# A decoder layer on one core: the order of ScalarE's work in the transposed attention, two more banks for the first pair's exponentials, and another order of the drain

## The chip, the core and the metric

The kernel runs on one core of a Trainium2 chip. The metric is the device time of one execution in microseconds (us). PE is the matmul engine, ScalarE (ACT), VectorE (DVE) and GpSimd (POOL) do the element-wise work, SyncE (SP) issues loads. Data is in SBUF; matmuls write PSUM, which has banks of 512 float32 per partition.

## The reference, cut to what is computed

```python
x = x + _L0_attn_ref(_layernorm(x), ...)          # bidirectional minGRU, x is (4, 512, 256)
x = x + _L0_xattn_ref(_layernorm(x), ctx, Wq, Wk, Wv)
x = x + _L0_ffn_ref(_layernorm(x), ...)           # product keys, 16 of 256 experts for each of 8 heads

def _L0_xattn_ref(x, context, Wq, Wk, Wv):        # context is (4, 1601, 256)
    q = einsum('bsd,ed->bse', x, Wq); k = einsum('btd,ed->bte', context, Wk); v = einsum('btd,ed->bte', context, Wv)
    attn = softmax(einsum('bse,bte->bst', q, k) * 256 ** -0.5, axis=-1)
    return einsum('bst,bte->bse', attn, v)
```

The change touches only the second line, the attention over the context.

## The kernel before

Three stages follow each other, `stage_gru`, `stage_attention` and `stage_ffn`; each engine runs its own program of the three, written out in order by hand, and semaphores are the only links between engines. All that follows is `stage_attention` (lines 599 to 1256).

**Tiling.** The 2048 tokens are 16 tiles of 128, worked in 8 pairs `p` (256 columns), two pairs a batch. Scores are computed transposed: 128 context positions are the partitions, 256 tokens the columns. The 1601 context positions are 13 tiles in 7 groups `j` (six of two tiles, one short one of 65 rows), so a group fills one PSUM bank. Float32 is carried by two float32r halves, high and low: the high half is a ScalarE copy, the low half what VectorE or GpSimd subtracts, and every product is three matmuls (`split_products`, L75 to L77).

**A pair.** In the score phase PE computes `scores(p, j)` for the 7 groups into three banks in turn, 12 matmuls a group; VectorE keeps a running maximum (L965, L968) and ScalarE copies the bank to SBUF (`read_scores`, L852), after which the bank is free. The maximum is turned and spread by PE (L1149, L1157). In the exponential phase, for each group: VectorE subtracts the maximum into one of the same three banks (`shift_scores`, L997), ScalarE takes Exp in place (`raise_scores`, L859) and copies the high half to SBUF (`probs_high`, L867), VectorE subtracts for the low half (`probs_low`, L1005), after which the bank is free. Meanwhile PE computes the values of the pair before (`value_group(p - 1, j)`, L1177 to L1179, 12 matmuls a group). `probs_high(p, j)` waits for that value group, since it overwrites its operand. `scores(p + 1, 0)` waits until the fifth group of pair p is subtracted, `scores(p + 1, 1)` and `(.., 2)` for the sixth and seventh.

**What stands between.** PE has a ring of two more banks (`pR[:, 1]` and `pR[:, 2]`) for items: X (transposes of the normalised rows of the next batch, L1206), Q (queries of the next batch), V (transposes of a pair's values, L1217) and O (a tile's output product). `before_scores` and `behind_values` place them; each item waits until the item two before it is out of its bank, which VectorE does last (`low` L944, `output` L950). `read_values` (L835) takes a pair's values out of their banks. The context of the next batch comes in 47 pieces through four raw slots: SyncE loads, ScalarE copies the high half (`piece_high`, L842), GpSimd subtracts (`piece_low`, L806), and then the slot is loaded again. `UPTO` says how many pieces are done by the end of each pair.

**ScalarE's order before** is in the program below: four pieces of a pair stand between score copies 1 to 4, the others in the exponential phase; there, Exp of the next group stands ahead of the halving of this one, and the values are read behind the sixth halving. VectorE shifts three groups, and then alternates subtraction and shift.

**The drain** is what follows the exponential phase of the last pair: V and two O of pair 6, the value groups of pair 7 with X for the next stage between, and the first queries of the next stage.

## Time and profile before

| | us |
|---|---|
| time, median of 3 runs | 455.24 |
| lowest and highest | 454.93, 456.31 |
| the profiled execution | 455.93 |
| its span | 453.5 |
| exponential phases of pairs 0 to 7 begin at | 96.5, 124.2, 156.4, 184.4, 211.9, 241.0, 267.6, 297.2 |
| first queries of the next stage begin at | 327.0 |

Times of rows are us from the span's start. The attention stage takes PE from 82 to about 332 us. The page counts an engine as busy while an instruction of it runs; idle time is put down to whatever released the next instruction.

### The profile page before, as it was taken

The page shows a single profiled execution, that of the slowest core. Times are in us where ns is not written, and L with a number is a line of the kernel's source. Part 1 is how long each engine was busy: PE and PEld are TensorE (multiplying, and loading weights), DVE is VectorE, ACT ScalarE, POOL GpSimd, SP SyncE. Part 2 cuts the span into 40 slices and gives each one's busy share as a digit, 9 for nine tenths or more (in the row PEclk, how much of TensorE's full clock was granted, in tenths as well). Part 3 has the DMA queues.
Part 4 walks back from the last instruction along what each step waited for, and adds up shares of the span by engine and source line. Part 5 has one row for each costly group of instructions (what it writes and reads, how often), then busy time and mean ns, then how long its engine had stood idle before and what let it go on. Part 6 is the DMA issues. An engine that isn't in the chain of part 4 may idle for free.

```text
span 453.5 us, 8077 instructions
## 1 busy us (share of the span) xinstructions
PE 405.5 (89%) x2680; PEld 374.8 (83%) x2680; DVE 318.8 (70%) x1093; ACT 268.5 (59%) x575; POOL 213.3 (47%) x212
## 2 busy tenths in 40 slices
PE   8999999984977969969699796974999999999887
PEld 7788888974977969969699795974987899999776
DVE  5787867756674656776557666665168698899997
ACT  3886685455574565566645655442146797778653
POOL 2799999602314224133331330200015675989994
PEclk9999999995996989999889898995999996999999
DMA  8601321020501204012130220000000000001011
GB/s 244 235 1 30 91 69 30 0 74 21 147 23 30 72 25 120 24 54 72 48 100 20 55 72 1 1 0 0 1 25 2 0 2 0 14 26 37 23 37 58
DMA packets 19992, 21.38 MB, mean 47 GB/s; under 512 B 3180, under 2 KB 16624, under 8 KB 19952
## 3 DMA queue, kind: packets, MB, share of 16 engines
q1 hardware_dynamic: 18832, 19.96, 15.0%
q10 hardware_dynamic: 1120, 0.92, 0.7%
q8 instruction: 21, 0.34, 0.3%
q14 instruction: 19, 0.16, 0.1%
HBM read 18.78 MB, written 2.10 MB: 46 GB/s over the span
## 4 chain that ended last, share of the span: by engine, by line
PE 57%; DVE 12%; POOL 10%; issue 8%; ACT 8%; DMA 2%; SPq 1%; ACTq 0%; DVEq 0%; POOLq 0%
PE keep_pQ L75 10%; PE keep_pQ L76 10%; PE keep_pQ L77 10%; POOL ffn_prod L1410 8%; DVE keep_pQ L997 5%; ACT att_pTh L867 5%; DVE att_pTl L1005 4%; ACT keep_pQ L859 3%; PE context_pR L534 2%; PE context_pA L534 2%; POOL ffn_near L1478 2%; DMA gru_wa<-in_xWk 2%; PE ffn_pK L1959 2%; PE ffn_pT L1989 1%; PE context_pR L1206 1%
## 5 line engine op out<-in xcount | busy, mean ns | idle before, releaser
L859 ACT ACTIVATE keep_pQ<-keep_pQ 128x512 f32<-128x512 f32 (+1 forms) x56 | 31.0, 553 | 58.7 <-DVE keep_pQ L997 58.6
L1005 DVE TENSOR_TENSOR att_pTl<-keep_pQ,att_pTh 128x512 fp32r<-128x512 f32 (+1 forms) x56 | 36.4, 652 | 39.8 <-ACT att_pTh L867 39.7
L852 ACT ACTIVATE att_prob<-keep_pQ 128x512 f32<-128x512 f32 (+1 forms) x56 | 31.4, 568 | 42.0 <-DVE att_most L965 15.7
L1410 POOL TENSOR_TENSOR ffn_prod<-ffn_first,ffn_near 128x1024 f32<-128x1024 f32 (+1 forms) x29 | 54.2, 1887 | 2.1 <-DVE ffn_first L1836 2.1
L75 PE MATMUL keep_pQ<-keep_qT0h,context_cTh 128*128 128x256 f32 (+1 forms) x104 | 32.4, 312 | 14.1 <-DVE att_pTl L1005 14.1
L75 PE MATMUL keep_pQ<-keep_qT0h,att_cTh 128*128 128x256 f32 (+1 forms) x104 | 33.2, 319 | 12.1 <-DVE att_pTl L1005 12.1
L968 DVE TENSOR_TENSOR att_most<-att_most,keep_pQ 128x512 f32<-128x512 f32 (+1 forms) x40 | 25.3, 633 | 23.4 <-PE keep_pQ L77 22.2
L997 DVE TENSOR_TENSOR keep_pQ<-att_prob,keep_pQ 128x512 f32<-128x512 f32 (+1 forms) x56 | 34.9, 649 | 6.5 <-PE keep_pQ L1157 6.5
L806 POOL TENSOR_TENSOR att_cNl<-keep_raw,att_cNh 128x512 fp32r<-128x512 f32 (+1 forms) x14 | 15.8, 1125 | 41.9 <-ACT att_cNh L842 41.9
L1989 PE MATMUL ffn_pT<-keep_ident,ffn_prod 128*128 128x128 f32 x240 | 30.4, 283 | 3.8 <-POOL ffn_prod L1410 3.8
L75 PEld LDWEIGHTS keep_pQ<-keep_qT0h,context_cTh 128*128 128x128 f32 (+1 forms) x104 | 21.3, 205 | 14.9 <-DVE att_pTl L1005 14.9
L1989 PEld LDWEIGHTS ffn_pT<-keep_ident,ffn_prod 128*128 128x128 f32 x240 | 28.6, 148 | 5.9 <-DVE ffn_hT L1869 4.9
L75 PEld LDWEIGHTS keep_pQ<-keep_qT0h,att_cTh 128*128 128x128 f32 (+1 forms) x104 | 21.7, 209 | 12.9 <-DVE att_pTl L1005 12.9
L76 PE MATMUL keep_pQ<-keep_qT0l,att_cTh 128*128 128x256 f32 (+1 forms) x104 | 31.7, 305 | 0.0
L77 PE MATMUL keep_pQ<-keep_qT0h,att_cTl 128*128 128x256 f32 (+1 forms) x104 | 31.6, 304 | 0.0
L867 ACT ACTIVATE att_pTh<-keep_pQ 128x512 fp32r<-128x512 f32 (+1 forms) x56 | 31.4, 563 | 0.0
L77 PE MATMUL keep_pQ<-keep_qT0h,context_cTl 128*128 128x256 f32 (+1 forms) x104 | 31.1, 299 | 0.0
L76 PE MATMUL keep_pQ<-keep_qT0l,context_cTh 128*128 128x256 f32 (+1 forms) x104 | 31.0, 298 | 0.0
L806 POOL TENSOR_TENSOR att_cTl<-keep_raw,att_cTh 128x512 fp32r<-128x512 f32 (+1 forms) x16 | 15.3, 971 | 31.7 <-ACT att_cTh L842 31.7
L1798 DVE MAX8 ffn_top<-ffn_e 128x8 f32<-128x32 f32 x256 | 29.3, 177 | 0.4 <-ACT ffn_e L1598 0.2
L235 POOL TENSOR_TENSOR gru_z<-gru_z,gru_g 128x512 f32<-128x512 f32 x16 | 26.5, 1656 | 6.4 <-DVE gru_g L414 5.7
L429 DVE TENSOR_TENSOR_SCAN gru_hT<-gru_c,gru_z 128x512 f32<-128x512 f32 x16 | 24.4, 1524 | 3.8 <-POOL gru_z L235 3.8
(356 smaller groups left out, 1413.0 us busy)
## 6 DMA issues: line engine op xcount, KB each, us to landing
keep_raw<-in_ctxT SPq DMA_DIRECT2D x24, 256.0 KB, 2.6
keep_raw<-in_ctx SPq DMA_DIRECT2D x24, 256.0 KB, 2.8
out<-keep_x SPq DMA_DIRECT2D x16, 128.0 KB, 1.7
keep_x<-in_x SPq DMA_DIRECT2D x3, 512.0 KB, 11.1
gru_wout<-in_W_out SPq DMA_DIRECT2D x1, 512.0 KB, 9.0
keep_raw<-in_fWq SPq DMA_DIRECT2D x2, 256.0 KB
keep_raw<-in_ctxT SPq DMA_DIRECT2D x8, 32.5 KB, 3.0
keep_raw<-in_ctx SPq DMA_DIRECT2D x4, 65.0 KB
```

The costliest lines, as they stand in the source:

```text
L75: pe.matmul(out, lh, rh, start=(i == 0), stop=False)
L76: pe.matmul(out, lh, rl, start=False, stop=False)
L77: last = pe.matmul(out, ll, rh, start=False, stop=(i == n - 1))
L806: pool.tensor_tensor(lo, raw(i % RAW), hi.bitcast(F32), ALU.subtract).then_inc(piece_lo, 1)
L852: act.activation(prob[0:rows(j), GROUPS[j][0]:GROUPS[j][-1] + 1].rearrange("p c n -> p (c n)"), pS[0:rows(j), score_bank(p, j), 0:n * COLS ...
L859: act.activation(e, e, ACT.Exp, scale=ATT_SCALE).then_inc(raised, 1)
L867: act.activation(to, pS[0:rows(j), exp_bank(p, j), 0:len(GROUPS[j]) * COLS], ACT.Copy).then_inc(prob_high, 1)
L997: dve.tensor_tensor(e, s, shift[0:rows(j)].unsqueeze(1).broadcast_to([rows(j), n, COLS]), ALU.subtract)\
L1005: dve.tensor_tensor(pT[1][0:rows(j), which], e, pT[0][0:rows(j), which].bitcast(F32), ALU.subtract)\
L1410: return eng.tensor_tensor(prod[:, i % PB, a:b].rearrange("p h (i j) -> p h i j", j=KEYS), (factor if factor is not None else first[:, n % ...
L1798: ins = dve.max(top[:, n % 2, t, h, a:a + 2 * TOPK], e[:, n % 2, t, h, half * KEYS:(half + 1) * KEYS])
L1989: last = pe.matmul(pW[:, i % 2, c * P:(c + 1) * P], prod[:, i % PB, h, c * P:(c + 1) * P], ident[:], start=(h == 0), stop=(c == 0 and h == ...
```

## The change

Five edits in `stage_attention`; no instruction is added or taken away.

- ScalarE in the exponential phase does Exp and halving of one group, then of the next, instead of Exp one group ahead; the values of the pair before are read behind the fifth halving instead of the sixth.
- ScalarE's pieces stand behind score copies 0 to 4, and what is left of a pair's pieces ahead of its first Exp; none is left in the exponential phase, save in pair 0. GpSimd's roots stand ahead of all pieces of their pair.
- In pairs 2 and 4 the items X stand one score group later.
- In pair 0, groups 4 and 5 are shifted into `pR[:, 0]` and `pR[:, 1]`, which are idle then; what waits for a bank of pair 0 waits for its last user in the new order. VectorE's two residual additions of that pair move towards its end.
- In the drain V(6), O(12), O(13) stand between the value groups of pair 7, and X of the next stage two groups later; ScalarE and VectorE follow in the same order.

```diff
@@ before_scores, behind_values
-        if j in (2, 3) and p in (1, 2, 4, 7):
-            out.append(("X", {1: 1, 2: 2, 4: 3, 7: 4}[p], j - 2))
+        if p in (1, 2, 4, 7):
+            first = 2 if p % 2 else 3
+            if j in (first, first + 1):
+                out.append(("X", {1: 1, 2: 2, 4: 3, 7: 4}[p], j - first))
...
         if p == PAIRS:
-            return {3: [("X", BATCH + 1, 0)], 4: [("X", BATCH + 1, 1)]}.get(j, [])
+            return {1: [("V", PAIRS - 2, 0)], 3: [("O", TILES - 4, 0)], 4: [("O", TILES - 3, 0)],
+                    5: [("X", BATCH + 1, 0)], 6: [("X", BATCH + 1, 1)]}.get(j, [])
@@ banks of the first pair; SPARE = (4, 5)
     def exp_bank(p, j):
-        return (2 * NG * p + NG + j) % BANKS
+        if p == 0 and j in SPARE:
+            return pR[:, SPARE.index(j)]
+        return pS[:, (2 * NG * p + NG + j) % BANKS]
+
+    def last_exp(p, j):
+        if p == 0:
+            return (1, 2, 6)[j]
+        return NG - BANKS + j
@@ scalar
         for p in range(PAIRS):
-            early, late = early_pieces(p), late_pieces(p)
+            left = list(pieces_at(p))
             for j in range(NG):
...
                 read_scores(p, j)
-                if early and j in (1, 2, 3, 4):
-                    piece_high(early.pop(0))
-            raise_scores(p, 0)
+                if p and j < 5 and left:
+                    piece_high(left.pop(0))
+            if p:
+                for i in left:
+                    piece_high(i)
             for j in range(NG):
-                if j + 1 < NG:
-                    raise_scores(p, j + 1)
+                raise_scores(p, j)
                 probs_high(p, j)
...
-                if p >= 1 and j == 5:
+                if p >= 1 and j == 4:
                     read_values(p - 1)
-                if p and j in (2, 4, 5) and late:
-                    piece_high(late.pop(0))
-            for i in late:
-                piece_high(i)
-        high(("V", PAIRS - 2, 0))
+            if p == 0:
+                for i in left:
+                    piece_high(i)
@@ vector
-            else:
+            elif p or j not in SPARE:
                 dve.wait_ge(prob_low, NG * p + j - BANKS + 1)
...
-                if p == 0 and j in (2, 4):
-                    last_residual((j - 2) // 2)
+                if p == 0 and j == 5:
+                    last_residual(0)
+            if p == 0:
+                last_residual(1)
@@ tensor
-                pe.wait_ge(prob_low, NG * (p - 1) + NG - BANKS + j + 1)
+                pe.wait_ge(prob_low, NG * (p - 1) + last_exp(p - 1, j) + 1)
...
+            if n == 0:
+                pe.wait_ge(prob_low, SPARE[1] + 1)
...
-        item(("V", PAIRS - 2, 0))
-        item(("O", TILES - 4, 0))
-        item(("O", TILES - 3, 0))
         for j in range(NG):
             value_group(PAIRS - 1, j)
             for it in behind_values(PAIRS, j):
```

ScalarE's program through the exponential phase of pair 2, before. L859 is Exp in place, L867 the halving, L842 a piece, L835 the reads of the values:

```order
L852 ACTIVATE att_prob<-keep_pQ 65x256
L859 ACTIVATE keep_pQ<-keep_pQ 128x512 x2
L867 ACTIVATE att_pTh<-keep_pQ 128x512
L859 ACTIVATE keep_pQ<-keep_pQ 128x512
L867 ACTIVATE att_pTh<-keep_pQ 128x512
L859 ACTIVATE keep_pQ<-keep_pQ 128x512
L867 ACTIVATE att_pTh<-keep_pQ 128x512
L842 ACTIVATE context_cTh<-keep_raw 128x512
L859 ACTIVATE keep_pQ<-keep_pQ 128x512
L867 ACTIVATE att_pTh<-keep_pQ 128x512
```

The same place in the changed kernel, where these lines are L856, L863, L871 and L846, through the third group:

```order
L856 ACTIVATE att_prob<-keep_pQ 65x256
L846 ACTIVATE context_cTh<-keep_raw 128x512 x2
L846 ACTIVATE context_cTh<-keep_raw 128x65
L863 ACTIVATE keep_pQ<-keep_pQ 128x512
L871 ACTIVATE att_pTh<-keep_pQ 128x512
L863 ACTIVATE keep_pQ<-keep_pQ 128x512
L871 ACTIVATE att_pTh<-keep_pQ 128x512
L863 ACTIVATE keep_pQ<-keep_pQ 128x512
L871 ACTIVATE att_pTh<-keep_pQ 128x512
```

The two Exp at the head are now one, and three pieces stand ahead of it.

VectorE's program in the exponential phase of pair 0, before. L997 is the shift, L1005 the subtraction, L1031 the residual addition:

```order
L1005 TENSOR_TENSOR att_pTl<-keep_pQ,att_pTh 128x512
L997 TENSOR_TENSOR keep_pQ<-att_prob,keep_pQ 128x512
L1031 TENSOR_TENSOR keep_x<-context_pR,keep_x 128x512
L1005 TENSOR_TENSOR att_pTl<-keep_pQ,att_pTh 128x512
L997 TENSOR_TENSOR keep_pQ<-att_prob,keep_pQ 128x512
L1005 TENSOR_TENSOR att_pTl<-keep_pQ,att_pTh 128x512
L997 TENSOR_TENSOR keep_pQ<-att_prob,keep_pQ 65x256
L1031 TENSOR_TENSOR keep_x<-context_pA,keep_x 128x512
L1005 TENSOR_TENSOR att_pTl<-keep_pQ,att_pTh 128x512
L1005 TENSOR_TENSOR att_pTl<-keep_pQ,att_pTh 65x256
```

The same place in the changed kernel, where these lines are L1001, L1009 and L1035:

```order
L1009 TENSOR_TENSOR att_pTl<-keep_pQ,att_pTh 128x512
L1001 TENSOR_TENSOR context_pR<-att_prob,keep_pQ 128x512
L1009 TENSOR_TENSOR att_pTl<-keep_pQ,att_pTh 128x512
L1001 TENSOR_TENSOR context_pR<-att_prob,keep_pQ 128x512
L1009 TENSOR_TENSOR att_pTl<-context_pR,att_pTh 128x512
L1001 TENSOR_TENSOR keep_pQ<-att_prob,keep_pQ 65x256
L1009 TENSOR_TENSOR att_pTl<-context_pR,att_pTh 128x512
L1035 TENSOR_TENSOR keep_x<-context_pR,keep_x 128x512
L1009 TENSOR_TENSOR att_pTl<-keep_pQ,att_pTh 65x256
L1035 TENSOR_TENSOR keep_x<-context_pA,keep_x 128x512
```

Shift and subtraction alternate as before; two groups lie in `context_pR`, and the residuals stand behind them.

PE's program at the start of the drain, before (L1177 to L1179 are values, L1217 is V, and L75 to L77 here are O):

```order
L1177 MATMUL context_pR<-att_cNh,att_pTh 128x258
L1178 MATMUL context_pR<-att_cNh,att_pTl 128x258
L1179 MATMUL context_pR<-att_cNl,att_pTh 128x258
L1217 MATMUL context_pR<-keep_ident,att_vn 128x128 x4
L75 MATMUL context_pR<-keep_WvTh,att_vTh 128x256
L76 MATMUL context_pR<-keep_WvTl,att_vTh 128x256
```

In the changed kernel V (L1226) has a value group of pair 7 (L1184 to L1186) ahead of it and behind it:

```order
L1184 MATMUL context_pR<-att_cNh,att_pTh 128x258
L1185 MATMUL context_pR<-att_cNh,att_pTl 128x258
L1186 MATMUL context_pR<-att_cNl,att_pTh 128x258
L1226 MATMUL context_pR<-keep_ident,att_vn 128x128 x4
L1184 MATMUL context_pA<-att_cNh,att_pTh 128x258
L1185 MATMUL context_pA<-att_cNh,att_pTl 128x258
```

V no longer stands directly behind the last value group of pair 6, and O no longer directly behind V.

## Rows read from the trace of the kernel before

**Rows 1.** The page, part 1: busy us, share of the span, instructions.

```profile
PE 405.5 (89%) x2680; PEld 374.8 (83%) x2680; DVE 318.8 (70%) x1093; ACT 268.5 (59%) x575; POOL 213.3 (47%) x212
```

**Rows 2.** The waits: engine, line, waited for; us in total, times, longest.

```profile
ACT keep_pQ L859 <- DVE keep_pQ L997: 58.6, 40, 3.3
PE keep_pQ L75 <- DVE att_pTl L1005: 26.1, 7, 8.1
PE context_pR L1217 <- ACT att_vn L835: 7.1, 2, 6.9
PE context_pR L1206 <- DVE att_xn L936: 4.1, 2, 3.0
```

**Rows 3.** Timeline of VectorE, pair 2; start us, us, engine, line, operation:

```profile
138.27 0.42 DVE L1005 TENSOR_TENSOR att_pTl<-keep_pQ,att_pTh 65x256 fp32r<-65x256 f32 x1 [0.64 <-ACT att_pTh L867]
...
156.43 1.89 DVE L997 TENSOR_TENSOR keep_pQ<-att_prob,keep_pQ 128x512 f32<-128x512 f32 x3 [0.98 <-PE keep_pQ L1157]
...
160.48 0.69 DVE L997 TENSOR_TENSOR keep_pQ<-att_prob,keep_pQ 128x512 f32<-128x512 f32 x1
...
162.32 0.69 DVE L1005 TENSOR_TENSOR att_pTl<-keep_pQ,att_pTh 128x512 fp32r<-128x512 f32 x1 [1.15 <-ACT att_pTh L867]
...
167.22 0.69 DVE L1005 TENSOR_TENSOR att_pTl<-keep_pQ,att_pTh 128x512 fp32r<-128x512 f32 x1 [1.15 <-ACT att_pTh L867]
```

**Rows 4.** Timeline of ScalarE, pair 2:

```profile
161.20 0.58 ACT L859 ACTIVATE keep_pQ<-keep_pQ 128x512 f32<-128x512 f32 x1 [1.36 <-DVE keep_pQ L997]
161.70 0.59 ACT L867 ACTIVATE att_pTh<-keep_pQ 128x512 fp32r<-128x512 f32 x1
```

**Rows 5.** Timeline of PE at the starts of pairs and of the drain:

```profile
108.06 0.58 PE L75 MATMUL keep_pQ<-keep_qT0h,context_cTh 128*128 128x256 f32 x1 [8.11 <-DVE att_pTl L1005]
...
143.91 1.09 PE L1206 MATMUL context_pR<-keep_ident,att_xn 128*128 128x128 f32 x4 [3.02 <-DVE att_xn L936]
...
163.40 0.28 PE L75 MATMUL context_pR<-keep_WvTh,att_vTh 128*128 128x256 f32 x1
163.52 0.28 PE L76 MATMUL context_pR<-keep_WvTl,att_vTh 128*128 128x256 f32 x1
...
167.96 0.58 PE L75 MATMUL keep_pQ<-keep_qT0h,att_cTh 128*128 128x256 f32 x1 [3.69 <-DVE att_pTl L1005]
...
195.93 0.39 PE L75 MATMUL keep_pQ<-keep_qT0h,context_cTh 128*128 128x256 f32 x1 [2.30 <-DVE att_pTl L1005]
...
313.18 0.55 PE L75 MATMUL context_pR<-keep_WvTh,att_vTh 128*128 128x256 f32 x1 [1.52 <-DVE att_vTl L944]
```

**Rows 6.** Windows; length, busy PE, PEld, DVE, ACT, POOL, granted clock, DMA, GB/s.

```profile
108.06:113.58 5.52, 5.52 (x28) 5.52 (x29) 3.67 (x13) 3.31 (x8) 3.48 (x3) 0.55 0.18 47
135.73:140.89 5.16, 5.16 (x28) 4.80 (x28) 3.25 (x12) 3.27 (x8) 2.37 (x3) 0.67 0.23 64
143.91:147.65 3.74, 3.74 (x21) 3.74 (x21) 1.28 (x4) 1.60 (x3) 1.18 (x1) 0.56 0.02 4
167.96:171.24 3.28, 3.28 (x17) 3.28 (x17) 2.10 (x6) 2.66 (x8) 2.06 (x2) 0.52 0.28 77
195.93:199.83 3.90, 3.73 (x28) 3.34 (x28) 2.33 (x6) 3.16 (x8) 2.20 (x2) 1.00 0.20 67
223.44:229.37 5.93, 5.93 (x28) 5.93 (x29) 3.18 (x9) 3.53 (x9) 2.65 (x3) 0.52 0.33 94
252.51:257.44 4.93, 4.93 (x28) 4.93 (x29) 1.96 (x4) 3.39 (x8) 2.19 (x2) 0.65 0.27 67
279.09:284.56 5.47, 5.09 (x28) 4.58 (x28) 4.38 (x13) 2.87 (x7) 0.00 (x0) 0.69 0.00 0
310.57:318.21 7.64, 6.12 (x29) 5.74 (x30) 4.45 (x15) 0.72 (x2) 0.39 (x1) 0.52 0.00 0
```

**Rows 7.** Timeline of GpSimd, the first four pieces:

```profile
110.10 4.04 POOL L806 TENSOR_TENSOR att_cTl<-keep_raw,att_cTh 128x512 fp32r<-128x512 f32 x4 [9.88 <-ACT att_cTh L842]
```

**Rows 8.** Loads by line: engine, operation, count, KB each, median us to landing.

```profile
keep_raw<-in_ctxT SPq DMA_DIRECT2D x24, 256.0 KB, 2.6
```

36 lines of the change are left out of this document (16 added, 20 removed).

## The prediction, made before the changed kernel ran

> **What bounds the kernel now.** I read first the page's busy times: PE is busy 405.5 us of the 453.5 us span, ScalarE 268.5 [rows 1]. So PE is the engine to fill, and the question is where its remaining time goes and at what clock it runs. The waits answer the first [rows 2]: the first scores of a pair waited 26.1 us in seven places for VectorE's subtraction L1005, the drain 7.1 us for ScalarE's reads of the values, the transposes of X 4.1 us for normalised rows; on the other side ScalarE's Exp waited 58.6 us in 40 places for VectorE's shift L997. Engines that are idle for each other in turn, while PE waits for the last of it: the exponential phase is a ring of latencies, not of work.
>
> The timeline of pair 2 shows the ring [rows 3, 4]. Write S(j) for the shift of group j, E(j) for Exp, H(j) for the halving copy, L(j) for the subtraction. VectorE ran S0, S1, S2 from 156.43; S3 began 160.48; E3 161.20 (0.72 behind S3, and ScalarE had been idle 1.36); H2 161.70 (0.50 behind E3, since H(j) stands behind E(j+1)); L2 162.32 (0.62); the next S comes one step of VectorE's queue after it, 0.60 to 0.61 (three shifts take 1.89, one 0.69). The turn is 0.72 + 0.50 + 0.62 + 0.61 = 2.45 us a group, and L4 began at 156.43 + 10.79 = 167.22. PE's last value group ended at 163.40, an output product of six matmuls followed to about 164.1, and pair 3 started at 167.96, after 3.69 idle [rows 5]. After such an idle stretch the granted clock is low: 0.52 to 0.69 over the first stretches of pairs 1 to 3, 5 to 7 and of the drain, 1.00 only behind one wait of 2.3 us [rows 6]; half the full 2.4 GHz is the 1.2 GHz level.
>
> **The change, part by part.**
>
> *ScalarE goes bank by bank* (E0 H0 E1 H1 ...). H(j) now stands right behind E(j) and waits for its result. No row shows an Exp followed by its own dependant. Its price lies between the issue step 0.50 and the duration plus a hand-over; an Exp lasts 0.58 [rows 4], and L follows H by 0.62 across engines, so I take 0.62, the upper neighbour. VectorE's order stays S0 S1 S2 L0 L1 S3 L2 S4 L3 S5 L4 S6 L5 L6, but S(j+1) is now done while ScalarE works on j. Counting from S0: E0 0.73, H0 1.35, L0 1.98; E1 1.84, H1 2.46, L1 3.09, S3 3.70; E2 2.95, H2 3.57, L2 4.31 (behind S3), S4 4.92; E3 4.43, H3 5.05, L3 5.68, S5 6.29; E4 5.65, H4 6.27, L4 6.90. So 1.29 us a group where there were 2.45, and L4 at +6.90 instead of +10.79. PE's values of the pair before end at 163.40, +7.0, in even pairs, and with an output product at +7.7; where two Q products lie between, PE's idle time was 2.30 instead of 3.69 [rows 5], so it is free 1.4 later, at +9.1. L4 is through at +7.65: the 26.1 us of waits at a pair's first scores go, save in the first pair. At 0.50 for the unseen step L4 comes 0.3 earlier and nothing more is won; at 0.8 it comes 0.5 later and costs even pairs 0.5 each.
>
> *What is late next.* The reads of the values move from behind H5 to behind H4. They wait for PE's last value group (+7.13 with its tail), take 0.27 each (estimated: half a copy step of 0.50, since they have half the columns), and E5, H5, E6, H6 stand behind them: E5 7.69, H5 8.31, L5 8.94, then the output O5 of even pairs on VectorE, done 10.07. PE has the next pair's first bank (1.4, 12 matmuls of 0.12 [rows 5]) from 7.7 to 9.1, and then its transposes of the values need O5's bank: 0.97 us of waiting. In odd pairs L5 is done 11.79 and PE is free 10.83: 0.96. So six transitions keep 0.97 each, 5.8 in all.
>
> *Pieces between score copies.* Each pair has up to five of its 7 or 8 context pieces at score copies 0 to 4 and the rest ahead of E0, where ScalarE was idle for up to 3.3 us [rows 2]. A piece is 0.5 of ScalarE's queue, and a step of the score phase is 1.4 to 1.8 of PE, so copy and piece (1.0) and even an X copy (1.5) fit. The fifth piece needs the raw slot of the first: 0.7 to GpSimd, 1.1 there (4.04 for three and a short one [rows 7]), 2.6 to load [rows 8], some 4.4, and it comes 7 us later. Hidden. If loads took three times as long it would no longer be.
>
> *X one copy later in pairs 2 and 4.* In pair 2 X came at 143.91, 5.64 behind L6 at 138.27 [rows 3, 5]: moments, GpSimd's root, four scalings. With L6 at +11.7 they come at +17.35; PE is ready at 14.6, so 2.7 us of its wait stays there, and the lower clock behind it (some 1.3). In pair 4 the wait goes. In pair 7, where X was not moved, the chain on VectorE is L6 at +9.95, O6 10.3, moments from 10.7, four scalings from 11.8 to 13.3 (steps as behind L6 in pair 2, without the root), and PE is ready at 11.85: 1.45 us, new.
>
> *First pair.* Groups 4 and 5 go to two idle banks, so pair 1's first two banks wait only for L1 and L2. S0 of pair 0 was 11.53 ahead of 108.06 (10.79, and 0.74 until the product), at 96.5, and L1 is now through at 96.53 + 3.84 = 100.4; PE was free at 108.06 - 8.11 = 99.95 [rows 5]. Waits that remain: 0.4; then X needs L5 (105.5) when PE is free at 103.2, 2.35; bank 2 needs L6 (106.5), behind which stand a residual, 0.55; and PE's fifth bank waits for ScalarE's second copy, which stands behind the fifth piece, whose load lands at about 109.9 (GpSimd's first piece starts about 4 us before 110.10 [rows 7] and takes 1.1; 2.6 more and ScalarE's hand-over), 1.5; turning the maxima 0.1. Together 4.9, and 0.4 of slow clock (little, since the fifth bank waits anyway).
>
> *Drain.* V(6), O, O now stand between the value groups of pair 7. They had cost 7.1 and 1.52 of idle PE [rows 2, 5]; in their place only value group 0 waits for the reads behind H4: 7.45 against 6.3, 1.2. All else has its operands, since V(6)'s halves are ready 1 us ahead of O.
>
> *Sum.* Taken away: 26.1 + 7.1 + 4.1 + 1.5 = 38.8 of waits; at each of the 12 waits another 0.16, since a matmul is shown 0.28 long and the next could start after 0.12: 1.9; and the low clock, one minus the granted share times the length of the stretches of rows 6: 2.5 + 1.7 + 1.65 + 1.6 + 0 + 2.85 + 1.7 + 1.7 + 2.9 (on its busy 6.1 us) = 16.6. Together 57.3. Left or new: 4.9 + 5.8 + 2.7 + 1.45 + 1.2 = 16.05, and 1.7 of clock: 17.75. Gain 39.5. The profiled execution took 455.93 us, so 416.4; it stood 0.7 above the median of 455.24, which makes 415.7.
>
> The clock term is the softest. Each pair still has a gap of about 1 us. Gaps of 2.33, 2.30 and 2.33 were followed by 0.67, 1.00 and 0.65 [rows 6]. None as short as 1 us stands in front of a slow stretch in these rows, so I let the clock stay high. The Trainium skill (TensorE: Matmul & The Clock Gate, section A second HAM failure mode) tells of a kernel that cycles through PSUM banks and idles briefly between groups of matmuls often enough that the clock swings between its two levels; by that rule the kernel would keep much of its 16.6 us, and the time would be near that of the second rival. No row here shows it without a wait of over 2 us ahead.
>
> **The rivals.**
>
> 1. *The ring turns slower than worked out:* E and H on ScalarE and S and L on VectorE all touch PSUM at once, or the step E to H costs 0.8 or more. Before, the pairs of them overlapped too, and durations stayed at 0.58 to 0.61 and 0.69, which speaks against it. At 0.2 to 0.3 more a group, L4 and the tail each come about 0.7 later in seven places: 5 us, 420.7.
>
> 2. *The clock still falls at the transitions.* For it: two of three gaps of 2.3 us did it, and the new gap stands close to the next one at X. Against it: work of 1.4 us now lies between. Price by rows 6: 1.6 us (the stretch at 167.96) in seven places, 11 us: 427.
>
> 3. *The moved pieces block the score copies,* and the kernel becomes slower. Place: copy 4 of pairs 1 to 5, behind it on ScalarE the copies on which PE's next banks wait. It decides from a load of 8 us (slack 5.6 beyond the 2.6 shown is 3); to eat 39.5 us over five pairs the fifth piece must come 7.9 us late each time, a load near 14 us. At 15 us: 5 x 9.4 = 47, and 463. Speaks against it: 2.6 us median over 24 loads [rows 8].
>
> 4. *The change doesn't do what it says:* H(j) is held by something else, such as PE's value groups, and the ring stays 2.45. H waits for the same value group as before; group 3 ends at 2.8 and 4 at 4.3 in even pairs, ahead of H. Then only X, drain and pieces count: some 14 us, 441.
>
> 5. *More is won:* no loss in the first pair (the load lands early) and no slow clock at all, 411.
>
> **How the numbers follow.** Forecast 415.7, own range 412 to 419: 0.60. Rival 1: 0.12; rival 2: 0.12; rival 3: 0.03; rival 4: 0.04; rival 5: 0.07; the rest, 0.02, no change. From 409 to 427.5 the range leaves out rivals 3 and 4, the rest and the ends. About 0.3% (1.4 us) is what a measurement of this kernel can tell from no change; every case but rival 3 and the rest is faster: 0.95, same 0.02, slower 0.03.
>
> **What would show it.** L4 begins 6.9 us behind S0 (was 10.8), H(j) starts 0.62 behind E(j). PE's wait for L1005 falls from 26.1 to about 6, most of it at the second bank of a pair instead of the first. The reads of the values after H4 wait for PE's value group. PE waits about 2.7 at X in pair 2 and 1.5 at X in pair 7. The drain runs without a wait over 1.5 us. The granted clock is 1.00 through the first banks of pairs 3 to 7. I am wrong in size if the first banks stay at 0.5 to 0.7 of the clock, and in kind if ScalarE idles in front of copy 4 for a piece's load.

## The result, and the profile after

The changed kernel took 417.92 us (median of 3 runs, 417.60 to 418.93) against 455.24 before: 0.918 of the time, 95% interval 0.9146 to 0.9214. The forecast was 415.7, its range 412 to 419. The profiled execution took 418.93 us with a span of 416.6, and is to be set against 455.93 and 453.5: 37.0 us less by the times and 36.9 by the spans, where the sum gave 39.5.

First the busy times, to be read against [rows 1], and the waits, against [rows 2] (engine, line, what it waited for; us in total, times, longest):

```profile
PE 390.8 (94%) x2680; PEld 357.8 (86%) x2680; DVE 321.1 (77%) x1093; ACT 271.3 (65%) x575; POOL 213.9 (51%) x212
```

```profile
ACT keep_pQ L863 <- DVE keep_pQ L1001: 21.7, 13, 3.3
PE context_pR L1215 <- DVE att_xn L940: 4.4, 2, 3.3
PE keep_pQ L75 <- DVE att_pTl L1009: 2.9, 5, 0.8
PE context_pR L1226 <- DVE keep_x L954: 2.5, 3, 0.8
PE context_pR L1215 <- DVE att_pTl L1009: 2.1, 1, 2.1
PE keep_pQ L1156 <- DVE att_top L979: 1.2, 1, 1.2
```

PE's wait for the subtraction at a pair's start (L1005 before, L1009 now) fell from 26.1 us to 2.9, its longest from 8.1 to 0.8; ScalarE's Exp waited for the shift 40 times before and 13 now. PE's busy time fell by 14.7 us at the same number of instructions, most of it by the clock. Of that, 11.8 us lie in the attention, from pair 0's first shift to the first queries of the next stage, first before and then changed (start and end; length, busy PE, PEld, DVE, ACT, POOL, granted clock, DMA, GB/s):

```profile
96.53:327.03 230.50, 191.20 (x1402) 185.28 (x1401) 142.47 (x285) 120.97 (x245) 54.03 (x54) 0.90 0.16 44
96.39:291.64 195.25, 179.40 (x1403) 172.50 (x1401) 141.47 (x279) 123.02 (x244) 53.70 (x53) 0.99 0.18 51
```

The shorter windows, to be read against [rows 6] (same columns): pair 7's first banks, the stretch behind pair 2's wait for X, and the drain:

```profile
253.94:258.40 4.46, 3.64 (x30) 3.29 (x28) 3.30 (x11) 3.49 (x8) 1.29 (x1) 1.00 0.00 0
138.57:143.90 5.33, 5.33 (x34) 5.33 (x35) 2.99 (x6) 3.73 (x8) 2.42 (x3) 0.70 0.35 97
279.60:285.00 5.40, 5.40 (x45) 5.40 (x46) 3.51 (x10) 2.19 (x5) 0.00 (x0) 1.00 0.00 0
```

Of eleven such stretches of the attention, at the places of rows 6 and behind the new waits, ten stand at 1.00 and one at 0.70.

The ring of the exponential phase, pair 6, first VectorE, then ScalarE (start us, us, engine, line, operation):

```profile
246.27 1.89 DVE L1001 TENSOR_TENSOR keep_pQ<-att_prob,keep_pQ 128x512 f32<-128x512 f32 x3 [0.98 <-PE keep_pQ L1164]
...
249.97 0.69 DVE L1001 TENSOR_TENSOR keep_pQ<-att_prob,keep_pQ 128x512 f32<-128x512 f32 x1
...
253.14 0.68 DVE L1009 TENSOR_TENSOR att_pTl<-keep_pQ,att_pTh 128x512 fp32r<-128x512 f32 x1
...
255.24 0.69 DVE L1009 TENSOR_TENSOR att_pTl<-keep_pQ,att_pTh 128x512 fp32r<-128x512 f32 x1 [1.09 <-ACT att_pTh L871]
```

```profile
247.00 0.58 ACT L863 ACTIVATE keep_pQ<-keep_pQ 128x512 f32<-128x512 f32 x1 [3.29 <-DVE keep_pQ L1001]
247.61 0.60 ACT L871 ACTIVATE att_pTh<-keep_pQ 128x512 fp32r<-128x512 f32 x1
248.11 0.59 ACT L863 ACTIVATE keep_pQ<-keep_pQ 128x512 f32<-128x512 f32 x1
...
253.43 0.39 ACT L839 ACTIVATE att_vn<-context_pA 128x258 f32<-128x258 f32 x1 [0.33 <-PE context_pR L1186]
```

The halving starts 0.61 behind its Exp, and the fifth subtraction 6.87 behind the first shift (253.14 - 246.27); in the kernel before it was 10.79 [rows 3]. In pairs 1, 3 and 5, where two query products stand between, it is 7.88.

Where the 36.9 us of span went, by the starts of the exponential phases: from that of pair 0 to that of pair 7 it was 200.6 us (297.17 - 96.53) and is 175.7 (272.07 - 96.39), 25.0 less; from there to the first queries of the next stage 29.8 and 19.5, 10.3 less; the next stage 1.5 less; up to pair 0, 0.1. The change doesn't touch the next stage. In the kernel before, the profiled execution has a stretch of 6.8 us at half the clock there (from 375.88) and the stage takes 126.5 us; the changed kernel has none and takes 125.0. The stage takes 126.3 to 126.6 us also in the profiles of `a1_exp_ahead`, `b4_read_late` and `d2_all`, and 124.9 in that of `a2_order_only`. So these 1.5 us come and go between profiled kernels; none of the edits is shown to cause them.

### The profile page after: what moved, and what is told of

Read it like the earlier page. It is cut to its first block, busy times and chain, and to the rows that moved or that the text cites. A ratio compares the mean times of both kernels' runs of the same rounds, so it can differ in the third digit from the quotient of the medians.

```text
span 416.6 us, 8078 instructions
## 1 busy us (share of the span) xinstructions
PE 390.8 (94%) x2680; PEld 357.8 (86%) x2680; DVE 321.1 (77%) x1093; ACT 271.3 (65%) x575; POOL 213.9 (51%) x212
## 4 chain that ended last, share of the span: by engine, by line
PE 67%; POOL 12%; DVE 8%; ACT 5%; issue 5%; DMA 2%; ACTq 0%; DVEq 0%; POOLq 0%
PE keep_pQ L75 10%; PE keep_pQ L77 9%; PE keep_pQ L76 9%; POOL ffn_prod L1416 8%; PE context_pR L534 3%; PE context_pA L1184 3%; PE context_pA L534 2%; PE context_pR L1186 2%; PE context_pR L1184 2%; PE context_pA L1186 2%; PE context_pA L1185 2%; PE context_pR L1185 2%; POOL ffn_near L1484 2%; ACT att_pTh L871 2%; ACT keep_pQ L863 2%
## 5 line engine op out<-in xcount | busy, mean ns | idle before, releaser
L856 ACT ACTIVATE att_prob<-keep_pQ 128x512 f32<-128x512 f32 (+1 forms) x56 | 31.2, 564 | 35.4 <-PE keep_pQ L77 10.5
L1009 DVE TENSOR_TENSOR att_pTl<-keep_pQ,att_pTh 128x512 fp32r<-128x512 f32 (+1 forms) x54 | 34.9, 647 | 14.9 <-ACT att_pTh L871 13.9
L863 ACT ACTIVATE keep_pQ<-keep_pQ 128x512 f32<-128x512 f32 (+1 forms) x54 | 30.3, 560 | 21.7 <-DVE keep_pQ L1001 21.7
L972 DVE TENSOR_TENSOR att_most<-att_most,keep_pQ 128x512 f32<-128x512 f32 (+1 forms) x40 | 25.3, 631 | 19.5 <-PE keep_pQ L77 18.2
L1001 DVE TENSOR_TENSOR keep_pQ<-att_prob,keep_pQ 128x512 f32<-128x512 f32 (+1 forms) x54 | 33.5, 648 | 5.7 <-PE keep_pQ L1164 5.7
L75 PE MATMUL keep_pQ<-keep_qT0h,context_cTh 128*128 128x256 f32 (+1 forms) x104 | 30.3, 291 | 2.8 <-DVE att_pTl L1009 1.4
L1995 PEld LDWEIGHTS ffn_pT<-keep_ident,ffn_prod 128*128 128x128 f32 x240 | 26.8, 141 | 6.6 <-DVE ffn_hT L1875 4.9
L871 ACT ACTIVATE att_pTh<-keep_pQ 128x512 fp32r<-128x512 f32 (+1 forms) x54 | 30.5, 566 | 2.8 <-PE context_pR L1186 1.2
L75 PE MATMUL keep_pQ<-keep_qT0h,att_cTh 128*128 128x256 f32 (+1 forms) x104 | 30.7, 295 | 1.5 <-DVE att_pTl L1009 1.5
L805 POOL TENSOR_TENSOR keep_rstd<-att_ve,keep_mhalf 128x4 f32<-128x4 f32 x3 | 3.3, 1089 | 56.0 <-DVE att_ve L1100 31.9
L76 PE MATMUL keep_pQ<-keep_qT0l,att_cTh 128*128 128x256 f32 (+1 forms) x104 | 29.7, 285 | 0.0
L77 PE MATMUL keep_pQ<-keep_qT0h,att_cTl 128*128 128x256 f32 (+1 forms) x104 | 29.6, 285 | 0.0
L77 PE MATMUL keep_pQ<-keep_qT0h,context_cTl 128*128 128x256 f32 (+1 forms) x104 | 29.2, 281 | 0.0
L76 PE MATMUL keep_pQ<-keep_qT0l,context_cTh 128*128 128x256 f32 (+1 forms) x104 | 29.1, 280 | 0.0
L75 PE MATMUL keep_pQ<-gru_xTh,gru_wh 128*128 128x512 f32 x56 | 24.0, 428 | 0.0
L75 PEld LDWEIGHTS keep_pQ<-keep_qT0h,context_cTh 128*128 128x128 f32 (+1 forms) x104 | 19.1, 184 | 4.2 <-DVE att_pTl L1009 2.3
## 6 DMA issues: line engine op xcount, KB each, us to landing
keep_x<-in_x SPq DMA_DIRECT2D x3, 512.0 KB, 10.3
```

The lines of the kernel that those rows point to most:

```text
L75: pe.matmul(out, lh, rh, start=(i == 0), stop=False)
L76: pe.matmul(out, lh, rl, start=False, stop=False)
L77: last = pe.matmul(out, ll, rh, start=False, stop=(i == n - 1))
L856: act.activation(prob[0:rows(j), GROUPS[j][0]:GROUPS[j][-1] + 1].rearrange("p c n -> p (c n)"), pS[0:rows(j), score_bank(p, j), 0:n * COLS ...
L863: act.activation(e, e, ACT.Exp, scale=ATT_SCALE).then_inc(raised, 1)
L871: act.activation(to, exp_bank(p, j)[0:rows(j), 0:len(GROUPS[j]) * COLS], ACT.Copy).then_inc(prob_high, 1)
```

## Experiments

Ratios are to the kernel before, measured beside it on the same chip; the changed kernel's is 0.918 (0.9146 to 0.9214). All through this section, "phases" is the time from the start of pair 0's exponential phase to that of pair 7 in the profiled execution: 200.6 us before, 175.7 changed. It leaves the drain out and shows smaller differences than the medians do, but it comes from one execution of each. "L5" and "L6" below are the sixth and seventh subtraction of a pair, as in the prediction.

### The order of ScalarE, undone and alone

`a1_exp_ahead`, changed kernel:

```diff
+            raise_scores(p, 0)
             for j in range(NG):
-                raise_scores(p, j)
+                if j + 1 < NG:
+                    raise_scores(p, j + 1)
                 probs_high(p, j)
```

> The changed kernel with one thing undone: ScalarE again raises group j + 1 before it halves group j; pieces, spare banks, reads and drain stay as changed. Theory (the order Exp, halving of one bank is what the change is worth): the shift of group j + 2 waits again for a bank that is one Exp longer in coming, the last subtraction of a pair moves from 6.87 us behind the first shift back towards 10.8, that is up to 3.9 us in each of 8 pairs, and the granted clock falls again behind the longer gaps on TensorE: 440 to 450 us. Rival (what ScalarE no longer does between the exponentials, pieces and reads, is what shortened them): at most 5 us is lost, 418 to 423 us.

450.62 us, ratio 0.9897 (0.9849 to 0.9946), 0.6 above the theory's range: 32.7 of the 37.3 us are gone with these lines (450.62 - 417.92). VectorE, pair 6:

```profile
268.81 1.89 DVE L1003 TENSOR_TENSOR keep_pQ<-att_prob,keep_pQ 128x512 f32<-128x512 f32 x3 [0.98 <-PE keep_pQ L1166]
...
279.60 0.69 DVE L1011 TENSOR_TENSOR att_pTl<-keep_pQ,att_pTh 128x512 fp32r<-128x512 f32 x1 [1.15 <-ACT att_pTh L871]
```

279.60 - 268.81 = 10.79, what the kernel before had, though neither pieces nor reads changed places. The rival (what ScalarE no longer does between the exponentials) is refuted. The granted clock of the run is 0.95 again. From pair 0's first shift to the next stage's first queries PE stands still for 35.1 us in place of 15.9, and is busy 14.0 us longer: more than half of what the order brings is waiting, and nearly all of the rest is the clock that falls behind the waits (159 matmuls start at the lower level there, 15 in the changed kernel).

`a2_order_only`, kernel before:

```diff
-            raise_scores(p, 0)
             for j in range(NG):
-                if j + 1 < NG:
-                    raise_scores(p, j + 1)
+                raise_scores(p, j)
                 probs_high(p, j)
```

> The kernel before with one thing done: ScalarE halves each group right behind its Exp. Pieces still stand between the exponentials and between the score copies 1 to 4, the reads of the values behind the last halving, pair 0 has no spare banks, and the drain is as before. Theory: the order alone brings most of the gain, less the pieces of ScalarE that stand in the exponential phase (three, some 0.6 us each) and the old drain (some 9 us): 426 to 436 us. Rival (order and pieces are only worth something together): over 440 us.

423.79 us, ratio 0.9311 (0.9275 to 0.9347): below the range of the theory. The order alone brings 31 us (0.069 of 455). Its phases take 172.8 us (269.41 - 96.59), 2.9 less than with all five edits. From pair 0 to pair 7, the other edits cost more than they bring. What it lacks stands in the drain (PE's waits):

```profile
278.31 1.09 PE L1215 MATMUL context_pR<-keep_ident,att_vn 128*128 128x128 f32 x4 [2.45 <-ACT att_vn L835]
281.32 0.55 PE L75 MATMUL context_pR<-keep_WvTh,att_vTh 128*128 128x256 f32 x1 [1.92 <-DVE att_vTl L942]
```

### The other edits, undone one at a time

`a3_pieces_back`, changed kernel, ScalarE's pieces in their old places:

```diff
-                if p and j < 5 and left:
+                if p and j in (1, 2, 3, 4) and left:
                     piece_high(left.pop(0))
...
                     read_values(p - 1)
+                if p and j in (2, 4, 5) and left:
+                    piece_high(left.pop(0))
```

> The changed kernel with ScalarE's pieces put back: behind the score copies 1 to 4 and behind the halvings 2, 4 and 5. Theory (each piece in the exponential phase lengthens it by its own duration, since ScalarE and VectorE now wait for each other there): of the three, the two in front of the fifth subtraction cost about 0.6 us each in the pairs that still have seven pieces: 2 to 6 us slower than the changed kernel. Rival (it is hidden by the ring of two banks): within 1 us of it.

418.54 us, ratio 0.9204 (0.9171 to 0.9236): no difference. Its phases take 174.6 us, 1.0 less. The theory is half right: in pairs 1, 3 and 5 L5 and L6 come later (11.58 and 12.78 behind the first shift, against 11.06 and 11.74), in pairs 2 and 4 by 0.5 and 0.7, and PE waits 1.16 to 1.27 us at the turns behind these five pairs and not 0.73 to 0.84. What makes up for it is the step from pair 0 to pair 1, 22.1 us against 24.0. There, and in the pairs behind, the way from the maximum over the groups to the first shift is 2.82 to 2.94 us, where the changed kernel has 3.2 to 3.7 in pairs 1 to 5. That led to the runs on GpSimd below.

`a4_drain_back`, changed kernel, the drain as before:

```diff
         if p == PAIRS:
-            return {1: [("V", PAIRS - 2, 0)], 3: [("O", TILES - 4, 0)], 4: [("O", TILES - 3, 0)],
-                    5: [("X", BATCH + 1, 0)], 6: [("X", BATCH + 1, 1)]}.get(j, [])
+            return {0: [], 3: [("X", BATCH + 1, 0)], 4: [("X", BATCH + 1, 1)]}.get(j, [])
...
+    ring += [("V", PAIRS - 2, 0), ("O", TILES - 4, 0), ("O", TILES - 3, 0)]
     for j in range(NG):
         ring += behind_values(PAIRS, j)
```

(and each engine's program follows that order).

> The changed kernel with the drain as before: the values of pair 6 and their two outputs stand whole ahead of pair 7's values, and the X products of the last tiles behind values 3 and 4. Theory, from the prediction's terms for the drain: TensorE waits 9 to 12 us more there in all (8.11 and 3.02 us were the two longest waits of this kind in the kernel before), the clock with it: 426 to 431 us. Rival (the next waits of the drain are late enough to take most of it back): under 3 us slower.

426.00 us, ratio 0.9373 (0.9334 to 0.9412), 8.1 us over the changed kernel by the medians; by the profiled spans 6.2, of which 5.1 lie behind pair 7's first shift and 1.3 in pair 2, where the low clock behind the X product lasts longer. The expectation took 8.11 and 3.02, which were waits of pairs 1 and 2, for those of the drain, 6.94 and 1.52. PE's waits in the drain come to 4.6 us against 1.07, 3.5 more and not 9 to 12, since with the faster ring V(6) waits 1.07 us and not 6.94; the wait that is left is for V's low half:

```profile
284.81 0.55 PE L75 MATMUL context_pR<-keep_WvTh,att_vTh 128*128 128x256 f32 x1 [3.52 <-DVE att_vTl L949]
```

`b1_no_spare`, changed kernel, no spare banks:

```diff
-        if p == 0 and j in SPARE:
-            return pR[:, SPARE.index(j)]
         return pS[:, (2 * NG * p + NG + j) % BANKS]
```

(and the waits for the banks' last users follow).

> The changed kernel without the two idle banks for pair 0's exponentials: groups 4 and 5 shift into the ring of three like the others. Theory: subtraction 4 of pair 0 comes some 1.5 to 2.5 us later and TensorE, which has little other work there, waits for it: 1.5 to 4 us slower than the changed kernel. Rival (the X products and the value products behind hide it): within 0.5 us.

418.98 us, ratio 0.9213 (0.9180 to 0.9246); phases 175.75 us, as in the changed kernel. By the phases the rival holds. PE waits once for a subtraction there, ahead of pair 1's first scores:

```profile
103.45 0.50 PE L75 MATMUL keep_pQ<-keep_qT0h,context_cTh 128*128 128x256 f32 x1 [4.18 <-DVE att_pTl L1005]
```

With the two banks it waits 0.42, 2.05, 0.27, 1.09 and 0.25 us in turn, 4.08 in all. The edit splits a wait and removes next to nothing.

`b2_x_back`, changed kernel:

```diff
-            first = 2 if p % 2 else 3
+            first = 2
```

> The changed kernel with the X products of pairs 2 and 4 one group earlier, where they stood before. Theory: the X product of pair 2, which waits 3.31 us for the scaled tile already, waits one group (about 1.4 us) longer, and pair 4's about as long as pair 7's (1.10 us): 1.5 to 4 us slower. Rival (TensorE waits less later for the same subtractions): within 0.7 us.

421.74 us, ratio 0.9265 (0.9234 to 0.9297), 3.8 us over by the medians; phases 177.6 us, 1.9 over. X in pair 2 waits 4.74 us in place of 3.31. By either measure the size is in the theory's range. Of the 1.9 us, 1.5 come in pair 2 and 0.4 in pair 4.

### What delays the first shift

The changed kernel's VectorE, and GpSimd at the same times:

```profile
116.63 1.32 DVE L979 TENSOR_TENSOR att_top<-att_most 128x256 f32<-128x256 f32 x1
...
136.20 2.22 DVE L940 TENSOR_SCALAR att_xn<-keep_x,keep_mv,att_rstd 128x256 f32<-128x256 f32 x4 [1.76 <-POOL att_rstd L799]
...
172.27 1.01 DVE L987 TENSOR_TENSOR att_diag<-keep_ident,att_mx 128x256 f32<-128x256 f32 x1
```

```profile
116.49 2.50 POOL L812 TENSOR_TENSOR att_cNl<-keep_raw,att_cNh 128x512 fp32r<-128x512 f32 x2 [1.59 <-ACT att_cNh L846]
...
136.13 1.18 POOL L812 TENSOR_TENSOR att_cNl<-keep_raw,att_cNh 128x512 fp32r<-128x512 f32 x1
...
171.81 2.51 POOL L812 TENSOR_TENSOR context_cNl<-keep_raw,context_cNh 128x512 fp32r<-128x512 f32 x2 [1.43 <-ACT context_cNh L846]
```

Where no piece of GpSimd runs beside them, the maximum over the groups (L979) and the diagonal (L987) take 0.42 us and the four scalings (L940) 1.38. In the kernel before, all eight maxima and all eight diagonals took 0.42 to 0.43; two of those maxima ran beside GpSimd's root of four values per partition, none beside a piece. Each long one begins inside a piece and ends behind it: the piece of 136.13 ends at 137.31, and the first scaling, begun at 136.20, took 1.26 us and not 0.40. The shifts, which read one operand in PSUM, keep their 1.89 for three beside the same pieces. So do the statistics of a tile, which read one operand in SBUF; this one runs inside the piece of 172.95 to 174.31:

```profile
173.20 0.41 DVE L959 BATCH_NORM_STATS2 att_stats<-keep_x 128x6 f32<-128x256 f32 x1
```

The Trainium skill (SBUF — State Buffer, section Who interferes with whom) has this: VectorE and GpSimd share one pair of SBUF ports as an exclusive lock, and a VectorE operation with two SBUF inputs contends with a GpSimd operation that reads SBUF. This trace agrees with it for the maximum and the diagonal: 0.72 to 1.32 us for the seven that began well inside a piece, and 0.42 to 0.43 for the others. The scalings read one tensor and two values per partition, and the first of them was held as well. To test that GpSimd's pieces are the cause, GpSimd alone was held:

`b3_hold_low`, changed kernel:

```diff
-            for i in pieces_at(p):
+            for n, i in enumerate(pieces_at(p)):
+                if p and n == 5:
+                    pool.wait_ge(shifted, NG * p + 1)
+                if p == 2 and n == 0:
+                    pool.wait_ge(xn_ready, 2)
                 piece_low(i)
```

> The changed kernel, except that GpSimd holds its leftover pieces (the sixth and seventh of a pair) until the first shift of that pair is done, and its first piece of pair 2 until the four scalings of that pair are done. No instruction is added on any computing engine. Theory (what was missed: VectorE's operations with two inputs in SBUF stand still while GpSimd works on SBUF; the maximum over the groups took 1.32 and 0.80 us beside pieces against 0.42, the diagonal 0.72 to 1.02 against 0.42, four scalings 2.22 against 1.38): these go back to 0.42 and 1.38 us, the way from the top to the first shift from 3.2 to 3.7 us back to 2.9, 2.5 to 3.2 us in all: 414.7 to 415.5 us. Rival (they are longer for another reason, such as reads of PSUM by both): the durations stay and the time with them, 417.9 us. Rival (held pieces come late for TensorE or hold the next pair): slower than the changed kernel.

416.94 us, ratio 0.9160 (0.9131 to 0.9189): by the medians not to be told from the changed kernel. Its phases take 174.0 us, 1.7 less. VectorE in pair 2:

```profile
135.98 1.38 DVE L944 TENSOR_SCALAR att_xn<-keep_x,keep_mv,att_rstd 128x256 f32<-128x256 f32 x4 [1.76 <-POOL att_rstd L799]
...
145.73 0.81 DVE L983 TENSOR_TENSOR att_top<-att_most 128x256 f32<-128x256 f32 x1
...
147.53 0.43 DVE L991 TENSOR_TENSOR att_diag<-keep_ident,att_mx 128x256 f32<-128x256 f32 x1
```

Scalings and diagonal are back to 1.38 and 0.43. The maximum over the groups stays at 0.81, and at 1.32 in pair 1: beside it runs the fifth piece (144.96 to 146.24 in pair 2), which this kernel doesn't hold. So the hold was placed one piece too late, and brought 1.7 us of the 2.5 to 3.2 expected. The mechanism stands: what GpSimd no longer runs beside is back to its length, and what it still runs beside is not.

### The reads of the values, and the clock

`b4_read_late`, changed kernel:

```diff
-                if p >= 1 and j == 4:
+                if p >= 1 and j == (4 if p == PAIRS - 1 else 5):
                     read_values(p - 1)
```

> The changed kernel, except that ScalarE reads the values of the pair before behind the last halving in pairs 1 to 6, and not behind the fifth. Theory (the five reads stand ahead of the sixth Exp, and VectorE waits 2.2 us there for the halving): the sixth subtraction comes earlier by the reads, and TensorE's wait of 0.75 to 0.97 us for it at each turn of pairs goes: up to 5 us faster, 413 to 415 us. Rival (the value products that wait for the two banks that the reads free come to stand in its place): between 0 and 3 us slower.

413.74 us, ratio 0.9092 (0.9060 to 0.9123), 4.2 us faster than the changed kernel; phases 171.0 us, 4.7 less. L5 comes 8.24 us behind the first shift in pairs 2, 4 and 6 (was 8.97) and about 9.2 in pairs 1, 3 and 5 (was 11.06); PE's waits of 0.73 to 0.84 at the second bank are gone. But X in pair 7 now waits 1.62 (was 1.10), since PE is there earlier. Reading the values behind H4, a part of the change, is a loss in pairs 1 to 6.

`c1_fill`, changed kernel:

```diff
+            if it == ("X", 2, 0):
+                pe.wait_ge(shifted, 2 * NG)
+                for _ in range(FILLS):
+                    pe.matmul(turned[:, 0], ident[:], ident[:], start=True, stop=True)
```

> The changed kernel with 12 more matmuls of the identity by itself in front of pair 2's first X product, started when the last shift of pair 1 is done, into a bank nobody reads; they fill the 3.31 us in which TensorE stands still there and compute nothing that is used. Theory (the granted clock of 0.70 between 138.57 and 143.90 us follows from that idle time): the clock stays 1.00 in the stretch behind it, which gives back some 1.6 us: 416 to 417 us. Rival (the clock falls there for another reason, or filling costs as much as it gives): the 0.70 stays, 417.9 us or up to 1 us more.

417.13 us, ratio 0.9163 (0.9133 to 0.9193); not to be told from the changed kernel by the medians, so the trace decides. The stretches in and behind the filled wait:

```profile
135.30:138.20 2.90, 2.35 (x22) 2.16 (x21) 2.58 (x5) 0.00 (x0) 1.43 (x2) 1.00 0.15 26
138.20:143.50 5.30, 5.30 (x48) 5.30 (x47) 4.27 (x9) 4.70 (x10) 3.13 (x3) 1.00 0.33 92
```

1.00 where there was 0.70, and 28.19 us from pair 1's first shift to pair 2's against 29.66: 1.5 us, as the clock term says. One execution could be chance, so the others count too: in each of the ten other profiled executions in which PE waits at this place (2.47 to 4.74 us) the clock falls to half there, and in `d1`, `d2` and `d3` below, where the wait is gone, it doesn't. The low clock there follows from the idle time and not from what runs behind it. The same profile has a low stretch that the changed kernel's has not, in pair 1, behind a first X product that waited equally long (2.05 and 2.04 us). Changed kernel, then this one:

```profile
105.37:111.31 5.94, 4.58 (x35) 4.13 (x36) 4.53 (x13) 3.32 (x8) 4.93 (x5) 1.00 0.39 97
```

```profile
104.73:110.20 5.47, 5.20 (x30) 4.96 (x31) 4.54 (x13) 3.10 (x7) 4.33 (x5) 0.69 0.37 96
```

It costs nothing visible (24.02 us from pair 0's first shift to pair 1's, against 23.96), since the wait for a score copy behind it, 1.09 us in the changed kernel, is gone in exchange.

### Towards a faster kernel

`d1_moments_early`, changed kernel: the statistics of the last four tiles leave the end of pair 1:

```diff
+                if p == 1:
+                    early_moments(j)
...
-            if p in (0, 1):
-                left_moments(2 + p)
-            if p == 1:
-                dve.tensor_scalar(ve[:, 2 * TPB:], mv2[:, 2 * TPB:, 1], LN_EPS, None, ALU.add).then_inc(ve_ready, 1)
+            if p == 0:
+                left_moments(2)
```

(`early_moments`: two statistics each at j = 3 and 4, aggregates and L1080's addition at j = 5.)

> The changed kernel with one thing moved on VectorE: the statistics of the last four tiles, which stand between pair 1's last subtraction and pair 2 (four at 130.81 us, the aggregates, the root on GpSimd behind them, 1.76 us of waiting for it), go between the maxima of groups 3 to 5 of pair 1. Theory (the 3.31 us wait of pair 2's X product is this chain): the four scalings stand directly behind pair 1's last subtraction, the wait goes to under 0.5 us and the clock of the stretch behind it to 1.00: 413 to 414.5 us. Rival (the X product then waits for something else, or the maxima of pair 1 come late by as much): 416 us or more.

415.87 us, ratio 0.9123 (0.9094 to 0.9152): a part of what the theory gave. The wait in pair 2 is gone, and from pair 1's first shift to pair 2's it is 24.8 us (was 29.7). But the step from pair 0 to pair 1 grew from 24.0 to 26.7. The clock fell to half there and pair 1's diagonal met a piece (1.01 us), but first of all VectorE now came late to the turn of the maxima:

```profile
PE keep_pQ L1173 <- DVE att_top L979: 2.4, 1, 2.4
```

`d2_all`: that, the late reads of b4, X one group later in pairs 1 and 7 (`first = 3`), and b3's hold from the fifth piece on (`n == 4`).

```diff
-            first = 2 if p % 2 else 3
+            first = 3
...
+                if p and n == 4:
+                    pool.wait_ge(shifted, NG * p + 1)
...
-                if p >= 1 and j == 4:
+                if p >= 1 and j == (4 if p == PAIRS - 1 else 5):
```

> The changed kernel with all that the runs so far point to: statistics early as in the run before, values read behind the last halving in pairs 1 to 6, X products of pairs 1 and 7 one group later, and GpSimd holding the fifth to seventh piece of a pair until that pair's first shift is done, so that none of them runs beside the maximum over the groups and the diagonal. Theory (the terms add): 4.2 us for the reads, 3.5 to 4.5 us for the statistics, 1.5 to 3 us for the held pieces, 1 to 3 us for the waits of 2.05 and 1.10 us in front of the X products: 404 to 409 us. Rival (one wait takes the place of another): 410 to 413 us.

411.75 us, ratio 0.9039 (0.9016 to 0.9062): by the rival's range. The terms don't add: the same lateness in pair 1 (2.5) stays, and PE's wait at score group 2 of pair 1 is 2.98. Moving X in pairs 1 and 7 brought nothing: in pair 1 the 2.98 stands in place of 2.05 and 0.27, and in pair 7 PE now waits twice for the same ring of two banks, in front of the output products, where `b4_read_late` waited 1.62 once:

```profile
254.50 0.39 PE L75 MATMUL context_pR<-keep_WvTh,att_vTh 128*128 128x256 f32 x1 [1.17 <-DVE keep_xT0l L952]
...
258.26 0.38 PE L75 MATMUL context_pR<-keep_WvTh,att_vTh 128*128 128x256 f32 x1 [1.38 <-DVE keep_xT0l L952]
```

From pair 6's first shift to pair 7's it is 27.2 us, against 25.6 in `b4_read_late`.

`d3_spread`: d2_all with VectorE's work around pair 1 spread:

```diff
+                if p == 1 and j in (2, 3):
+                    early_moments(at, 3 * TPB + 2 * (j - 2), 2)
...
+            if p == 0:
+                last_residual(0)
+                last_residual(1)
```

(with the first four tiles' statistics at the maxima 1 to 3 of pair 1.)

> The run before (d2_all) with VectorE's work around pair 1 spread out. There, the statistics between the maxima of pair 1 made TensorE wait 2.47 us for the maximum over the groups, and the last subtraction of pair 0 at 105.46 us, behind one half of the last residual, made it wait 2.98 us. Now both halves of that residual stand behind pair 0's last subtraction, the statistics of the first four of the eight tiles between the maxima of groups 1 to 3 of pair 1 (VectorE stood idle 1.36 and 1.86 us there), and those of the last four between the subtractions 2 to 4 of pair 1, beside TensorE's query products. Theory (VectorE has room there, and the waits were its lateness): 0.6 us less in front of score group 2 of pair 1, up to 2 us less in front of the turned maxima: 408.5 to 410.5 us. Rival (the ring of pair 1 has no room, and the statistics only move the wait to pair 1's last subtractions): 411 to 413 us.

411.06 us, ratio 0.9038 (0.9009 to 0.9068): 0.7 below d2_all by the median and equal by the interval; the phases are 167.1 us against 169.0. The profiled execution took 410.32, in the theory's range, the median not. It is the fastest kernel here by the median, 1.6% under the changed one, and it keeps the 27.3 us from pair 6 to pair 7: by the 25.6 of `b4_read_late`, leaving X where it was in pair 7 should give another 1.7 us (an estimate, not run). Of its waits on PE and of VectorE in pair 2:

```profile
PE keep_pQ L75 <- DVE att_pTl L1013: 3.6, 3, 2.5
PE keep_pQ L1179 <- DVE att_top L983: 1.1, 1, 1.1
```

```profile
141.67 0.43 DVE L983 TENSOR_TENSOR att_top<-att_most 128x256 f32<-128x256 f32 x1
...
143.19 0.43 DVE L991 TENSOR_TENSOR att_diag<-keep_ident,att_mx 128x256 f32<-128x256 f32 x1
```

With the fifth piece held too, the maximum over the groups is back to 0.43, which b3 had left open.

## Why the prediction was right, and where it was off

**The ring: right.** The measured 417.92 us lies in the range of 412 to 419, 2.2 above the forecast, and for the reason given. The step from Exp to halving was 0.61 (0.62 taken), the fifth subtraction at +6.87 (6.90). a1 and a2 show by undoing and by doing that this edit alone carries 31 to 33 us. The rival of a slower ring and that of a ring held at 2.45 are out. In pairs 1, 3 and 5 L4 was at +7.88: the query products were not worked into those steps, and it cost nothing, since PE was free only later.

**The clock: right in place, priced too high.** 1.7 us of low clock were to stay; what stayed is (1 - 0.70) x 5.33 = 1.6. The second rival, that gaps of 1 us let it fall, is out: behind 0.75, 0.82 and 1.10 us it stood at 1.00. So the swing of the clock that the Trainium skill (TensorE: Matmul & The Clock Gate, section A second HAM failure mode) tells of, weighed in the prediction, is not seen here with gaps this short. c1 shows that the one slow stretch belongs to its 3.31 us gap. But the changed kernel's first X product waited 2.05 us and kept the clock, while in the profiles of a3, a4, b4, c1 and d1 the clock fell behind the same wait; that the changed kernel kept it there was luck, though not worth much. The price is treated under the sum.

**What is late next: right in place.** Predicted and measured waits of PE: six transitions at the second bank 5.8, and 4.7 (three of about 0.74, three of 0.82 to 0.84); X in pair 2 2.7, and 3.31; X in pair 7 1.45, and 1.10; first pair 4.9, and 5.3; drain 1.2, and 1.07, with 0.2 more at the last output. Together 16.05, and 15.7. The near agreement is in part luck, since it hides two misses that cancel. The transitions came out 1.1 smaller than worked out. And VectorE was held by GpSimd: 0.84 us in the scalings ahead of X in pair 2, 0.9 at the turn of pair 1, where 0.1 was forecast and 1.21 came. The prediction had moved the pieces and asked only whether ScalarE and the loads have room; it did not ask beside what GpSimd's half of a piece then runs.

**The sum: 4.2 us too large, and 1.6 us of luck.** The sum is of the attention alone. It gave 39.5; the attention became 230.50 - 195.25 = 35.25 us shorter. The profiled time fell by 37.0 only because 1.6 us more went elsewhere, 1.5 of it in the next stage, by a low stretch of the clock that no edit is shown to have removed. Three terms were off, by the windows and the trace:

- *Idle time* fell by 39.3 - 15.85 = 23.45 us, where 38.8 - 16.05 = 22.75 was forecast: 0.7 more.
- *The tails.* "At each of the 12 waits another 0.16" was taken away, and nothing put back for the waits that are left or new. There are 15 of them in the attention, where there were 12 (those over 0.2 us), so the term is not 1.9 gained but 3 x 0.16 = 0.5 lost: 2.4 less.
- *The clock's price.* It was one minus the granted share, that is half of each low stretch. These are two matmuls in a low stretch of the kernel before:

```profile
313.53 0.42 PE L76 MATMUL context_pR<-keep_WvTl,att_vTh 128*128 128x256 f32 x1
313.75 0.42 PE L77 MATMUL context_pR<-keep_WvTh,att_vTl 128*128 128x256 f32 x1
```

They start 0.21 to 0.22 us apart, and at the full clock 0.12 [rows 5], so the low level costs 44% of its time in this kernel and not 50%. Counted by the matmuls that start in low stretches, 149 of them in the attention before and 15 changed, the clock gave (149 - 15) x 0.094 = 12.6 us (0.213 less 0.119 each), where 16.6 - 1.7 = 14.9 was forecast: 2.3 less.

That is 39.5 + 0.7 - 2.4 - 2.3 = 35.5, against 35.25 measured; the rest stays open. This is arithmetic on the two traces; no run tested the tails by themselves.

**Edits priced too kindly.** The five edits were summed as if each brought its own part. The runs say otherwise: spare banks nothing that can be told (b1), ScalarE's pieces nothing (a3), the early reads a loss of 4 (b4), X later 2 to 4 (b2), the drain 5 to 8 (a4), the order 31 to 33 (a2, a1). By the medians, each undone alone, they sum to 32.7 - 4.2 + 3.8 + 8.1 = 40.4 us and not to 37.3; no run tells overlap from the noise of five medians. The prediction had all the numbers for the reads (they stand ahead of E5 and cost 0.97 at six transitions) and took them as given by the change, which is right for its time; it did not say that this edit was the cause. For the first pair, it gave the waits that remain and didn't compare them with those without the edit.

**Open.** b1's median stands 1.1 us above the changed kernel's; the intervals overlap and the profiled phases are equal, so no difference is shown, and one of about 1 us is not excluded. What each edit is worth is measured from one side, undone from the changed kernel; only ScalarE's order was also tried alone.

## What to carry to other kernels

Where two engines alternate on the same buffers, put each step right behind its producer, and count the ring's turn from the timeline before moving work; here the order of two steps carried five sixths of the gain. When a sum credits something for every wait removed, debit the same for every wait that stays, and take the price of a low clock from matmuls at either level. Compare the sum with the stretch of the kernel that it is about, not with the whole time, which can agree by luck. Before moving a GpSimd piece, look at which VectorE operations it will run beside: here those that read two or more operands from SBUF paid, and those with one operand in PSUM, or a single one in SBUF, did not.
